# Decayed k and q of a head: four long GpSimd products in its first part, or fourteen short ones in the recurrence of the head before

## The reference, cut to what matters

```python
def step(S, xs):                         # per value head, S is 128 x 128
    qt, kt, vt, gt, bt = xs
    S = S * jnp.exp(gt)[..., None, None]
    kS = jnp.einsum('bhk,bhkv->bhv', kt, S)
    S = S + bt[..., None, None] * kt[..., :, None] * (vt - kS)[..., None, :]
    o = jnp.einsum('bhk,bhkv->bhv', qt, S)
    return (S, o)
conv = sum((xp[:, i:i + T, :] * conv_w[:, i] for i in range(KC)))   # of x @ W_qkv, then silu
q = _l2norm(q) * DK ** (-0.5); k = _l2norm(k)
o = o * jax.lax.rsqrt(mean(o * o) + 1e-06) * norm_w * _silu(z)      # then @ W_out
```

## Time and profile before

| | us |
|---|---|
| median of three runs (2117.54 to 2123.35) | 2123.1 |
| the profiled execution, device time | 2117.74 |
| its span | 2115.8 |
| TensorE busy | 1917.6 (91%) |
| VectorE busy | 1505.7 (71%) |
| ScalarE busy | 984.2 (47%) |
| GpSimd busy | 759.0 (36%) |

### The profile page before, as it was taken

One profiled execution on the slowest core, in us unless ns is written; L12 is line 12 of the kernel. 1 busy time (PEld: TensorE's weight loads), 2 busy tenths in 40 slices (PEclk: granted clock), 3 DMA queues, 4 the chain that ended last, 5 costly groups with the idle time before them and its releaser, 6 DMA issues.

```text
span 2115.8 us, 43478 instructions
## 1 busy us (share of the span) xinstructions
PE 1917.6 (91%) x15082; PEld 1402.3 (66%) x15082; DVE 1505.7 (71%) x2430; ACT 984.2 (47%) x2535; POOL 759.0 (36%) x685
## 2 busy tenths in 40 slices
PE   4578886888799999999999999999999999999998
PEld 3246662333555687877878778787687777877877
DVE  5786771111677687787787877878778787787887
ACT  1012224777213354645545455455564555645544
POOL 4730002110300334616336164362543624526343
PEclk9689998999899999999999999999999999999999
DMA  6635661000122200010010000100001001010010
GB/s 245 209 91 200 184 178 55 26 20 1 55 60 70 82 17 35 5 35 30 15 35 10 30 30 15 35 30 10 30 15 35 30 10 40 5 35 30 15 45 20
DMA packets 75254, 111.75 MB, mean 53 GB/s; under 512 B 23318, under 2 KB 56742, under 8 KB 72006
## 3 DMA queue, kind: packets, MB, share of 16 engines
q1 hardware_dynamic: 71694, 102.32, 15.1%
q0 software_dynamic: 3072, 8.39, 1.3%
q10 hardware_dynamic: 446, 0.48, 0.1%
HBM read 85.80 MB, written 28.52 MB: 54 GB/s over the span
## 4 chain that ended last, share of the span: by engine, by line
PE 51%; DVE 16%; issue 4%; ACT 3%; POOL 0%; DVEq 0%; ACTq 0%; POOLq 0%
PE ps L1273 5%; PE ps L1311 4%; PE ps L1321 4%; DVE conv L1862 3%; DVE P L2034 3%; DVE P_term L2031 3%; PE ps L1544 3%; PE ps L1493 3%; PE ps L1533 3%; PE ps L1428 3%; PE ps L1417 3%; PE ps L1546 3%; PE ps L1520 2%; PE ps L1450 2%; PE ps L1525 2%
## 5 line engine op out<-in xcount | busy, mean ns | idle before, releaser
L1862 DVE SCALAR_TENSOR_TENSOR conv<-raw,tap_st,conv 128x1024 f32<-128x1024 f32 x204 | 299.5, 1468 | 3.6
L1273 PE MATMUL ps<-xnT,w_conv_st 128*128 128x512 f32 x544 | 247.6, 599 | 0.0
L1842 POOL TENSOR_TENSOR o<-o,silu_z 128x256 f32<-128x256 f32 x128 | 138.5, 1082 | 255.5 <-DVE silu_z L1882 141.7
L816 DVE TENSOR_REDUCE m_part<-ps 128x1 f32<-128x640 f32 (+7 forms) x176 | 176.4, 1027 | 67.1 <-PE ps L667 53.5
L1726 POOL TENSOR_TENSOR gmask_Q<-upto,g 128x2048 f32<-128x2048 f32 x17 | 61.4, 3611 | 363.5 <-PE ps L1500 335.5
L998 ACT ACTIVATE probs<-ps 128x1024 f32<-128x1024 f32 (+7 forms) x256 | 145.9, 660 | 58.1 <-PE ps L933 28.7
L1273 PEld LDWEIGHTS ps<-xnT,w_conv_st 128*128 128x128 f32 x544 | 98.9, 191 | 101.1 <-issue 96.2
L1565 ACT COPY raw<-ps 128x512 f32<-128x512 f32 x136 | 80.7, 594 | 173.4 <-PE ps L1273 173.4
L1822 POOL TENSOR_TENSOR kq_decayed<-conv,decay_rows 128x1024 f32<-128x1024 f32 x64 | 159.3, 2521 | 0.0
L1321 PE MATMUL ps<-w_z_st,xnT 128*128 128x256 f32 x512 | 148.8, 393 | 0.0
L903 POOL DMA_INDIRECT slot_outputs<-scratch_slots_y,token_slots x32 | 30.6, 958 | 310.9 <-POOLq L496 202.0
(11 more groups left out here) (345 smaller groups left out, 4728.9 us busy)
## 6 DMA issues: line engine op xcount, KB each, us to landing
decay_rows<-scratch_egc SPq DMA_DIRECT2D x17, 1024.0 KB, 4.7
w_conv_st<-in_w_conv SPq DMA_DIRECT2D x17, 512.0 KB, 3.3
scratch_slots_x<-yacc SPq DMA_DIRECT2D x8, 1024.0 KB, 14.9
slot_rows<-scratch_slots_x SPq DMA_DIRECT2D x16, 512.0 KB, 4.7
scratch_slots_y<-slot_outputs SPq DMA_DIRECT2D x16, 512.0 KB, 3.4
w_gate_up<-in_gu SPq DMA_DIRECT2D x8, 768.0 KB
w_gate_up<-in_gu SPq DMA_DIRECT2D x32, 192.0 KB
kq_decayed<-in_gu SPq DMA_DIRECT2D x22, 256.0 KB, 2.8
```

Of the source, the lines that this page charges most:

```text
L816: dve.tensor_reduce(dst, src, AX.X, ALU.max).then_inc(s_max, 1)
L1273: mm = pe.matmul(ps[:, 6 + n % 2, :], wc[:, k, (n // 2) * P:(n // 2 + 1) * P], m.xnT[:, k, (n % 2) * HALF:(n % 2 + 1) * HALF], start=k == ...
L1842: g.tensor_tensor(oc, oc, zs[:, c, :], ALU.mult).then_inc(s_oz, 1)
L1862: op = dve.scalar_tensor_tensor(out=cv[:, t, :], in0=raw[:, t, at:at + T], scalar=tap[:, t, at:at + 1], in1=cv[:, t, :], op0=ALU.mult, op1 ...
```

## The change

The four long products go. In their place stands `decayed(c)`, two products for chunk c (one for each value head, q and k in one instruction, 128x256), called for chunks 1 to 7; chunk 0 has no state before it and is never read. GpSimd calls it in the recurrence of the head before: `decayed(c)` once that head's last reader of the chunk is done (the state matmul of step c, for chunk 7 the output matmul), followed by the gated product of chunk c-1. The next head's scalars move behind `decayed(6)`, the first `rsqrt_outputs` stands behind `decayed(4)`, `totals` goes to the end. For the first head the seven calls stand before the loop. The next head's masked gates also wait for its k convolution. SyncE loads the first `decay_rows` in expert unit 12, and each next one at the top of the loop body behind the seventh chunk, ahead of the weights. As `kq_decayed` is now in use during the expert units, their buffers move to `decay_P` and `k_nat_decayed`, and the layer's input, read back at the end, moves from `decay_rows` to `row_of_block`.

```diff
-        x_in = egr[:].rearrange(...)
+        x_in = row[:].rearrange(...)
-        th = floats(kq_room, 0, 2 * HALF, "b t", b=2)
-        gs = floats(kq_room, 2 * HALF, 2 * HALF, "b t", b=2)
-        hid = floats(kq_room, 4 * HALF, 2 * HALF, "b t", b=2)
-        wgu = floats(kq_room, 6 * HALF, 2 * HALF, "b k g n", b=2, k=KT, g=2)
+        th = floats(ep_room, 0, 2 * HALF, "b t", b=2)
+        gs = floats(ep_room, 2 * HALF, 2 * HALF, "b t", b=2)
+        hid = floats(ke_room, 0, 2 * HALF, "b t", b=2)
+        wgu = floats(ke_room, 2 * HALF, 2 * HALF, "b k g n", b=2, k=KT, g=2)
...
+                if u == 12:
+                    sp.wait_ge(s_egst, 48)
+                    decay_rows(m.egc_rows[0:2, :])
...
-            sp.wait_ge(s_egst, 48)
-            decay_rows(m.egc_rows[0:2, :])
             with sp.Fori(0, NK) as i:
+                sp.wait_ge(s_kqe, i * 7 + 7)
+                decay_rows(m.egc_rows[bass.ds(2 * i + 2, 2), :])
                 sp.wait_ge(s_pj, i * 8 + 8)
...
-                sp.wait_ge(s_kqe, i * 4 + 4)
-                decay_rows(m.egc_rows[bass.ds(2 * i + 2, 2), :])
-            sp.wait_ge(s_egr, 16 * (NK + 1))
+            sp.wait_ge(s_rk, NK * 5)
...
                 pe.wait_ge(s_pt, i * ND + ND)
+                pe.wait_ge(s_kqe, i * 7 + 7)
...
+            def decayed(c):
+                at = slice(c * P, (c + 1) * P)
+                for e in range(2):
+                    op = g.tensor_tensor(kqe[:, e, :, at], cv[:, 0:2, at], egr[:, e, at].unsqueeze(1).broadcast_to([P, 2, P]), ALU.mult)
+                op.then_inc(s_kqe, 1)
...
+            pool.wait_ge(s_cvd, 2)
+            pool.wait_ge(s_egr, 16)
+            passed()
+            for c in range(1, NC):
+                decayed(c)
...
-                pool.wait_ge(s_egr, i * 16 + 16)
-                passed()
-                for e in range(2):
-                    for a in range(2):
-                        g.tensor_tensor(kqe[:, e, a, :], cv[:, a, :], egr[:, e, :], ALU.mult).then_inc(s_kqe, 1)
...
                 pool.wait_ge(s_x, i * ND + ND)
+                pool.wait_ge(s_cvd, i * 4 + 6)
                 gmask(i + 1)
                 pool.wait_ge(s_ot, i * 4 + 4)
...
-                for c in range(NC):
-                    if c == 5:
+                def gate_z(c):
+                    pool.wait_ge(s_var, i * 16 + 2 * c + 2)
+                    pool.wait_ge(s_zs, i * NC + c + 2)
+                    oc = o[:, c].rearrange("p e n -> p (e n)")
+                    g.tensor_tensor(oc, oc, zs[:, c, :], ALU.mult).then_inc(s_oz, 1)
+
+                pool.wait_ge(s_egr, i * 16 + 32)
+                for c in range(1, NC):
+                    if c < NC - 1:
+                        pool.wait_ge(s_su, i * 14 + 2 * c + 1)
+                    else:
+                        pool.wait_ge(s_aw, i * NC + NC)
+                    passed()
+                    decayed(c)
+                    if c == 6:
                         pool.wait_ge(s_vn, i * 2 + 2)
                         pool.wait_ge(s_hm, i * 3 + 3)
                         scalars(i + 1)
-                    pool.wait_ge(s_var, i * 16 + 2 * c + 2)
-                    if c == NC - 1:
-                        totals(i + 1)
-                    pool.wait_ge(s_zs, i * NC + c + 2)
-                    oc = o[:, c].rearrange("p e n -> p (e n)")
-                    g.tensor_tensor(oc, oc, zs[:, c, :], ALU.mult).then_inc(s_oz, 1)
-                    if c % 4 == 3:
-                        rsqrt_outputs(i, c // 4)
+                    gate_z(c - 1)
+                    if c == 4:
+                        rsqrt_outputs(i, 0)
+                gate_z(NC - 1)
+                rsqrt_outputs(i, 1)
+                totals(i + 1)
...
-                dve.wait_ge(s_kqe, i * 4 + 4)
+                dve.wait_ge(s_kqe, i * 7 + 7)
                 more(4)
```

More of the change, by code:

```diff
@@ L1130, in stage_l1 @@
         y = m.x
-        x_in = egr[:].rearrange("p e t -> p (e t)").rearrange("p (c d) -> p c d", d=D)
+        x_in = row[:].rearrange("p k n -> p (k n)").rearrange("p (c d) -> p c d", d=D)
         tanh_moe = xs[:].rearrange("p e c n -> p (e c n)")
@@ L1138, in floats @@
             return ap.rearrange("p (" + shape + ") -> p " + shape, **dims) if shape else ap
-        kq_room = kqe[:].rearrange("p e a t -> p (e a t)")
+        ep_room = e_p[:].rearrange("p e c n -> p (e c n)")
+        ke_room = ke[:].rearrange("p e c n -> p (e c n)")
         ua_room = ua[:].rearrange("p e c a i -> p (e c a i)")
         zs_room = zs[:].rearrange("p c n -> p (c n)")
-        th = floats(kq_room, 0, 2 * HALF, "b t", b=2)
-        gs = floats(kq_room, 2 * HALF, 2 * HALF, "b t", b=2)
-        hid = floats(kq_room, 4 * HALF, 2 * HALF, "b t", b=2)
-        wgu = floats(kq_room, 6 * HALF, 2 * HALF, "b k g n", b=2, k=KT, g=2)
+        th = floats(ep_room, 0, 2 * HALF, "b t", b=2)
+        gs = floats(ep_room, 2 * HALF, 2 * HALF, "b t", b=2)
+        hid = floats(ke_room, 0, 2 * HALF, "b t", b=2)
+        wgu = floats(ke_room, 2 * HALF, 2 * HALF, "b k g n", b=2, k=KT, g=2)
         w3f = floats(ua_room, 0, 768, "c s", c=NC)
```

## The result

The changed kernel takes 2110.3 us (median of eight runs, 2106.0 to 2114.3), the kernel before, in eight runs beside it, 2122.2 (2117.5 to 2125.1). The ratio is 0.9944, 95% interval 0.9931 to 0.9957: faster by 11.9 us. I had forecast 2120, less than 0.3% from the time before; the measured time is inside the range (2107 to 2133), but outside the forecast's own case. What came true is the milder form of rival A (chance 0.32), which for a lag of 2.6 us gave 2112; the lag is 2.52.

What follows compares the result with a forecast made beforehand. The head loop was taken as TensorE's. Per head 1.14 - 1.56 = -0.42 us, times 15 is -6.3; with +3.1 at the end and +0.5 for weights, -2.7: 2120 us, between 2107 and 2133.

Steps and rivals of the forecast that it cites:

- the forecast's own case: A GpSimd lag at the head's end between 2.9 and 3.7 us, giving 2117 to 2130 us; chance 0.47.
- rival A: Smaller lag, from less collision and 0.65 us multiplies: 2.3 us gives 2108, 2.6 gives 2112; chance 0.32 for lags under 2.9.
- the lag: How much later than before GpSimd ends the second rsqrt at the head's end; put at 3.1 us.
- Taken away, 1.56 us a head: At the head's start VectorE no longer stands behind long GpSimd multiplies, nor TensorE for VectorE: 23.4 us over 15 heads.
- Added in the recurrence, hidden: Multiplies of 0.70 us, 1.4 a chunk, fit beside VectorE's PSUM-fed work for chunks 1 to 4, delaying nothing.
- Rival B: In step 4 chunk 3's product loses its race with the convolution step: lag 3.9 to 4.0, 2134 us; chance 0.20.
- the collision with the convolution step: VectorE's last convolution step falls into GpSimd's head scalars and delays them by 0 to 1.22 us, taken as 0.8.
- Slack 1.96, stand 1.14: At L1300's second half TensorE has 1.96 us before the lag reaches it, so it stands 1.14 us per head.
- The end, +3.1: After the last head the lag goes through whole to the last output tile: +3.1 us, once.
- Weights, +0.5: The decayed rows' load queues before expert unit 13's weights: 0.5 us of stall, between 0 and 2.7, once.
- At nothing: the gates' wait: The masked gates' new wait costs nothing, the k convolution being done before matmuls they await anyhow; bound 0.5 us in all.
- the 3.3 us of lag by that rule: If the convolution step waits out the power, then holds GpSimd up by about 1.0: stand 1.34, -3.3 us over 15 heads.

Runs made afterwards that it cites:

- e5: The kernel before with the four long GpSimd products left out (decayed k and q never made): ratio 0.9892 to the kernel before, 2097.98 us beside 2118.54.
- e2: The changed kernel with chunk 7's two products moved into the next head, behind the last rsqrt: ratio 0.9893 to the kernel before, 2065.05 us beside 2085.33.
- e9: The changed kernel with one more, unread, 128x256 product ahead of chunk 7's: ratio 1.0011 to the kernel before, 2087.50 us beside 2085.47.
- e4: The changed kernel with two more, unread, 128x256 products ahead of chunk 7's: ratio 1.0116 to the kernel before, 2111.29 us beside 2085.33.
- e3: The changed kernel with the first decayed-rows load issued between an expert's gate-up and down weights: ratio 0.9932 to the kernel before, 2072.77 us beside 2085.33.
- e6: The changed kernel with the wait for the k convolution set behind the masked gates: ratio 0.9945 to the kernel before, 2107.18 us beside 2118.54.
- e1: The kernel before with its four long products cut into fourteen of 128x256 in their old place: ratio 0.9886 to the kernel before, 2063.5 us beside 2085.3.
- e7: The changed kernel with the edits of e2 and e3 together: ratio 0.9907 to the kernel before, 2097.89 us beside 2118.54.
- e10: The edit of e4 on the changed kernel, run once more: ratio 1.0136 to the kernel before, 2113.94 us beside 2085.47.

## Why the prediction was right in its mechanism and wrong in its size

- *Taken away, 1.56 us a head.* Right. e5 gives 1.55, and L1450's wait is gone. One thing in the same stretch was not in the sum: the first 24 matmuls of the output projection (L1311, now L1313) took 5.45 us in head 7 before, and take 5.34 behind the new stand; 5.45 again in e2, which has no stand. I take the 0.11 us for short waits for ScalarE's `xn_nat`, which the new stand covers; no row shows them as such.
- *Added in the recurrence, hidden.* Right. The multiplies take 0.70 us, begin with the S updates, and the product of chunk 3 starts as they end (1391.33), 0.15 us before the convolution step. The steps keep 3.65 us. Rival B, which lives of that race, didn't occur: in no head was it lost.
- *The lag, 3.1 us: the mis-sized term.* It is 2.52. Of its terms, the collision with the convolution step was put at 0.8 and is 0.4: the step (L1893) starts at 1401.19, inside the power that runs from 1400.11 to 1401.77, and takes its plain 1.22 us; the power keeps its 1.66, and only the next scalar, begun at 1401.85, takes 0.62 in place of 0.20, to the end of the step. The two multiplies of chunk 5 were put at 2.5 us from 1396.66 (1395.28 in this frame). GpSimd's first multiply started at 1395.24, 0.07 ahead of VectorE's L1912, which then took 1.74; the pair took 2.39. So GpSimd, which I had coming second, came first and the pair was done 0.15 us sooner. The two make 0.55 of the 0.57 us. The prediction had the step fall on the power, as it did, and took from the multiplies that one of the two would stand; it held against rival A that GpSimd without idle would collide nearly everywhere.
- *Slack 1.96, stand 1.14.* The slack was right, to 0.03 (2.52 - 0.54, 3.20 - 1.21), and e9 and e4 show the slope. The stand is 0.56 for the lag alone. -1.56 + 0.56 - 0.11 + 0.08 (gates) = -1.03 a head, as measured; forecast -0.42. The 0.61 a head are the 9 us by which the sum missed.
- *The end, +3.1.* It is the lag, whatever that is: from the last head's first gate matmul to L1912 1.48 us more, and with the 1.03 of that head's beginning, 2.5.
- *Weights, +0.5.* 1.7 in this execution, 1.4 of it the wait, within the bounds of 0 and 2.7. The wait and its removal by e3 show the mechanism. I had put the added delay at 2.5 us, from the landing times of two sizes; from the issue of the weights to their use it was 662.73 - 656.81 = 5.9 us, 3.1 more than their median landing.
- *At nothing: the gates' wait.* 1.2 us in all, over the bound of 0.5 (e6).

Sum: -15.4 + 2.5 + 1.7 = -11.2, and -11.9 +- 2.8 by the runs. Had the lag been put at 2.5, the same steps would have given 2111. The forecast's own case (0.47) asked for a lag of 2.9 to 3.7 and didn't come; A (0.32) did, and of A's two reasons one, and that in part: the collision cost less, but the multiplies kept their 0.70. So the steps were right, and the time lies in the range because the range took in a smaller lag, not because 2120 was near.

Two slips of the prediction change nothing here: with a lag of 2.3 the heads of rival A give 15 x (0.3 - 1.56) = -18.9 and not -18, so 2107 and not 2108; and B's 2134 lies just outside the stated range.

The prediction took two rules from the Trainium skill (SBUF — State Buffer, Who interferes with whom), both wider than they stand there. A VectorE instruction with at most one SBUF input is said there to stay clear of GpSimd outside the two-port modes alone; L2023, a copy with one SBUF input, did stand here (1.85 us in place of 0.29). And that whoever starts first holds the shared pair for the whole instruction is said there of those modes; of an instruction with two SBUF inputs the section says that it contends with a GpSimd instruction that reads SBUF. For the multiplies this case's traces agree with both (2.46 us before, 0.83 in e1). For a GpSimd power of 128x8 they don't: the convolution step with two SBUF inputs began 1.1 us into it and kept its 1.22 us. So the 3.3 us of lag by that rule were further off than the 3.1 us of the sum.

## What to carry to other kernels

Where a short VectorE instruction stands behind a long GpSimd one, cut the GpSimd instruction before you move it: e1 got back, in the old place, about twice what the move did (0.9886 against 0.9944 and 0.9956), though one head of its trace took 91 us, which none did in the nine traces with the products moved. When work is moved to an engine that is then without idle, ask who waits for the last thing this engine makes and by how much that is early; up to that slack the move is free (e2), above it each 0.7 us costs 0.7 in every head (e9, e4). What isn't needed by then is put behind it in the queue, as in e2 and e7, and a load that isn't needed yet behind those that are.

## What the runs showed of the hardware that I had not expected

*A VectorE instruction can miss its turn many times.* In e1's long head L2019, which takes 0.94 in the median, took 5.73 us (VectorE, GpSimd, TensorE):

```profile
1712.98 5.73 DVE L2019 TENSOR_TENSOR U<-U,half_mask_a 128x512 f32<-128x512 f32 x1
```

```profile
1708.53 9.63 POOL L1823 TENSOR_TENSOR kq_decayed<-conv,decay_rows 128x256 f32<-128x256 f32 x14
```

```profile
1719.22 5.94 PE L1450 MATMUL ps<-U,row_of_block 128*128 128x240 f32 x30 [3.85 <-DVE U L2021]
```

GpSimd's products end at 1718.16, and VectorE's instruction half a microsecond later: it stood through the seven or so that were left, though in the other heads it got in after the one that was running (0.94 us, 0.25 over its plain 0.69). TensorE stood 3.85 us, L1450 took 5.94 in place of 4.17, and the granted clock was down here too:

```profile
1719.00:1722.00 3.00, 2.78 (x14) 2.74 (x14) 2.30 (x7) 0.00 (x0) 0.00 (x0) 0.75 0.91 330
1722.00:1725.00 3.00, 3.00 (x19) 3.00 (x19) 2.43 (x8) 0.00 (x0) 0.00 (x0) 0.68 0.05 19
```

The grant is short by (0.25 + 0.32) x 3 = 1.7 us, as behind the stands of e4. In 16 heads it happened once, and why there stays open.

*The clock falls after a stand of 1.9 us, and not every time:* 9 and 11 heads of 14, 3.4 us at 1.2 GHz, 1.68 us a head. That is 15 and 18 us in the profiled executions, more than half of the 26 and 28 by which e4 and e10 are slower than the kernel before; the stands alone cost 87.15 - 86.83 = 0.32 a head.

*A power on GpSimd didn't keep VectorE out:* 1.22 us for a step of two SBUF inputs that began inside one of 1.66, in every head of the changed kernel (1.22 to 1.23).
